# A hybrid transformer block: turned tiles in groups of four, a longer lead in the expert stage, and gathers issued singly

## The reference, cut to what matters

```python
x = x + attn_a(ln(x))   # rope attention, 16 heads of 8
x = x + ffn(ln(x))
x = x + attn_b(ln(x))   # covariance attention, 16 heads of 8
x = x + ffn(ln(x))
# ffn: h = x + attention(layer_norm(x)); h + moe_ff(layer_norm(h))
def moe_ff(x, w_gate, w1, b1, w2, b2):
    t = x.reshape(B * T, D)                          # 2048 rows of 128
    tw, ti = lax.top_k(softmax(t @ w_gate), 2)       # of 8 experts
    tw = tw / jnp.sum(tw, axis=-1, keepdims=True)
    for e in range(8):
        we = jnp.sum(jnp.where(ti == e, tw, 0.0), axis=-1)
        h = gelu(t @ w1[e] + b1[e]) @ w2[e] + b2[e]  # 128 -> 512 -> 128
        out = out + we[:, None] * h
```

## Time and profile before

| | |
|---|---|
| median of 3 runs | 967.03 us (964.18 to 973.73) |
| profiled execution | 970.91 us |
| its span | 969.1 us |
| PE busy | 803.9 us (83%) |
| ACT, DVE, POOL busy | 576.6, 545.4, 481.1 us |
| PE's mean granted clock | 0.871 |
| mixture of phase 1 | 328.6 to 482.4 us |
| mixture of phase 2 | 798.5 to 941.4 us |

### The profile page before, as it was taken

How to read it: one execution, slowest core, us unless ns; L and a number is a source line. 1 busy time by engine, 2 the same in 40 slices (tenths; PEclk the granted TensorE clock), 3 DMA queues, 4 the chain that set the end, 5 groups by cost and what they waited for, 6 DMA issues and landing times.

```text
span 969.1 us, 21562 instructions
## 1 busy us (share of the span) xinstructions
PE 803.9 (83%) x7166; PEld 574.7 (59%) x7166; DVE 545.4 (56%) x1370; ACT 576.6 (60%) x1336; POOL 481.1 (50%) x906
## 2 busy tenths in 40 slices
PE   2999999999985983879878989999998599666780
PEld 2755556666652783878745556666665258566680
DVE  4799988788872230023656768788887322210122
ACT  1377767878752681555555556787876248444460
POOL 6667777577635215045444456366763621412305
PEclk9999989999965896889978889999998558878895
DMA  9200000000001452555200000000000124435552
GB/s 288 68 3 2 3 2 3 3 3 3 3 13 34 121 155 84 134 147 147 59 13 13 14 13 2 3 2 3 3 3 5 42 75 126 132 101 154 145 135 65
DMA packets 58746, 56.31 MB, mean 58 GB/s; under 512 B 7944, under 2 KB 43536, under 8 KB 58640
## 3 DMA queue, kind: packets, MB, share of 16 engines
q1 hardware_dynamic: 40288, 39.13, 15.0%
q0 software_dynamic: 4096, 8.40, 3.0%
q10 hardware_dynamic: 14256, 7.41, 2.6%
HBM read 40.10 MB, written 14.29 MB: 56 GB/s over the span
## 4 chain that ended last, share of the span: by engine, by line
PE 56%; DVE 17%; POOL 8%; issue 7%; another core or an unknown queue 7%; ACT 4%; DMA 1%; ACTq 1%; POOLq 0%; DVEq 0%; SPq 0%
PE bankO L456 11%; DVE M L1112 9%; PE bankE L697 8%; PE bankR L710 8%; PE bankE L475 7%; PE bankE L429 6%; PE bankR L442 3%; POOL Yg L1610 3%; DVE QKV L1074 2%; PE bankE L466 2%; ACT G L951 2%; PE bankR L526 2%; PE bankR L544 2%; PE bankR L496 1%
## 5 line engine op out<-in xcount | busy, mean ns | idle before, releaser
L1112 DVE TENSOR_REDUCE M<-bankR 128x2 f32<-128x512 f32 x512 | 326.5, 684 | 113.1 <-PE bankR L442 76.9
L838 ACT ACTIVATE Pr<-bankE 128x512 f32<-128x512 f32 x512 | 276.9, 595 | 128.2 <-PE bankE L429 119.8
L442 PE MATMUL bankR<-KQ 32*128 32x256 f32 x1024 | 181.6, 349 | 17.5 <-DVE M L1112 13.7
L456 PE MATMUL bankO<-Pr,Vx 128*32 128x256 f32 x2048 | 179.7, 427 | 5.9 <-ACT OT L832 5.9
L429 PEld LDWEIGHTS bankE<-KQ 32*128 32x128 f32 x1024 | 85.3, 199 | 108.7 <-issue 72.4
L1327 DVE COPY Yb<-bankR 128x128 f32<-128x128 f32 x92 | 26.6, 290 | 208.7 <-PE bankR L710 137.5
L429 PE MATMUL bankE<-KQ 32*128 32x256 f32 x1024 | 141.6, 350 | 1.7 <-issue 0.6
L951 ACT ACTIVATE G<-bankE,W 128x128 f32<-128x128 f32 x368 | 105.0, 371 | 56.7 <-PE bankE L697 35.6
L442 PEld LDWEIGHTS bankR<-KQ 32*128 32x128 f32 x1024 | 117.2, 198 | 32.2 <-DVE M L1112 27.3
L710 PE MATMUL bankR<-w,G 128*128 x736 | 107.9, 294 | 27.0 <-ACT G L951 23.7
L1610 POOL DMA_INDIRECT Yg<-sorted_y,SLOT x64 | 61.8, 966 | 126.6 <-DMA sorted_y<-Yb 97.3
(11 more groups left out here) (169 smaller groups left out, 1169.4 us busy)
## 6 DMA issues: line engine op xcount, KB each, us to landing
W<-in_w1b SPq DMA_DIRECT2D x92, 258.0 KB
XT<-sorted_u SPq DMA_DIRECT2D x92, 64.0 KB
sorted_y<-Yb ACTq DMA_DIRECT2D x92, 64.0 KB
sorted_u<-Yg SPq DMA_DIRECT2D x2, 1472.0 KB, 9.6
KQ<-MT SPq DMA_DIRECT2D x128, 4.0 KB
X<-in_x SPq DMA_DIRECT2D x8, 128.0 KB, 6.5
sorted_u<-U,SLOT POOLq DMA_INDIRECT x64
Yg<-sorted_y,SLOT POOLq DMA_INDIRECT x64
```

Of the source, the lines that this page charges most:

```text
L442: k = mm(dve_bank("raw", layer, b, h)[:, z * T:z * T + T], QT[rows, kb, g, z * P:z * P + P], KT[rows, kb, g, :], start=True, stop=True)
L456: k = mm(bankO[SL * j:SL * j + SL, cols], Vx[:, b % VB, kc, HG * g + j, :], Pr[:, g % 2, j, kc, :], start=(g % 2 == 0 and kc == 0), stop=( ...
L838: nc.scalar.activation(Pr[:, (h // HG) % 2, h % HG], act_bank("S", layer, b, h).rearrange("p (k q) -> p k q", k=TT), ACT.Exp, scale=EXP_SC ...
L1112: v.tensor_reduce(M[:, b % 2, :, h], dve_bank("raw", layer, b, h).rearrange("p (t k) -> p t k", t=TT), AX.X, ALU.max, negate=True).then_in ...
```

## The change

- The tiles are turned in groups of XG = 4 (the last group of a half has 3), 6 groups to a half. SP loads a group with one DMA, PE turns its tiles into one bank of bankE, ACT copies the bank at once. XT and XTT hold two groups.
- PE's `hidden` runs LEAD = 3 tiles ahead of `outputs`, ACT's gelu two ahead; G holds 5 tiles, W 7, Yb 6. ACT stores tile `at - 4`. Each half begins anew with two turned groups and three `hidden`.
- SP asks for W 7 tiles ahead across the border of the halves, and for the second half's first groups at tile 18.
- `timely` goes: block 5 has its gate in step 18, blocks 6 and 7 in `drain`. `first_rows` and `name_tiles` are one with `sort_rows`. For half 0, `do_rank` part 0 stands at the end of step 17 and part 1 with the sort in step 18; the scatter of half 0 follows step 18. For half 1 all stand one tile later.
- In the steps, `do_uT`, `do_gate`, `choose` and `weigh` stand somewhat later on every engine. In `fill`, seven pairs of raw scores and maxima stand at tiles 16 to 22 of the second half, combines of blocks 2 and 3 at 17 and 20.
- The four gathers of a covariance step are issued one by one: before `stack_k`, after it, after `stack_v` and after `norm`.

```diff
@@ -40,7 +40,13 @@
 GROUPS = HB * TT * 2
 NTL = (GROUPS * P + E * (P - 1)) // P
 NAT = 2 * NTL
-NX, NW, NY, NYG = 6, 5, 3, 8
+LEAD = 3
+LAG = 4
+NXG, NW, NGB, NY, NYG = 2, 7, 5, 6, 8
+XG = 4
+GROUP = [(half * NTL + i, min(XG, NTL - i)) for half in range(2) for i in range(0, NTL, XG)]
+NGRP = len(GROUP)
+GROUP_OF = {first: q for q, (first, _) in enumerate(GROUP)}
 
 
...
 
-        def timely(u):
-
-            return None if u and LAYERS[u[0]] == "ffn" and u[1] >= NB - 3 else u
+        def group_at(at):
+
+            return GROUP_OF.get(at + XG + 2) if at % NTL + XG + 2 < NTL else None
+
+        def group_of(at):
+
+            q = max(q for q, (first, _) in enumerate(GROUP) if first <= at)
+            return q, at - GROUP[q][0]
...
 
-            def load_x(ph, at):
-
-                half, i = divmod(at, NTL)
-                k = (ph * NAT + at) % NX
+            def load_x(ph, q):
+
+                half, i = divmod(GROUP[q][0], NTL)
+                n, k = GROUP[q][1], (ph * NGRP + q) % NXG
                 if i == 0:
                     sp.wait_ge(scattered[half], 16 * GROUPS * (ph + 1))
-                need(sp, x_turned, ph, at - NX)
-                sp.dma_start(XT[:, k], sorted_u[half][i * P:i * P + P, :]).then_inc(x_in[k], 16)
+                need(sp, x_turned, ph, q - NXG)
+                sp.dma_start(XT[:, k, 0:n, :],
+                             sorted_u[half][i * P:(i + n) * P, :].rearrange("(j p) d -> p j d", p=P)).then_inc(x_in[k], 16)
 
             def load_w(ph, at):
...
                         set_shift(*m, 0)
-                def begin(half):
-                    for i in range(NW - 1):
-                        load_w(ph, half * NTL + i)
-                    for i in range(NX - 1):
-                        load_x(ph, half * NTL + i)
-
-                for half in range(2):
-                    begin(half)
-                    for i in range(NTL):
-                        at = half * NTL + i
-                        if i + NX - 1 < NTL:
-                            load_x(ph, at + NX - 1)
-                        if i + NW - 1 < NTL:
-                            load_w(ph, at + NW - 1)
+                for at in range(NW):
+                    load_w(ph, at)
+                for q in range(2 * NXG):
+                    load_x(ph, q)
+                for at in range(NAT):
+                    if at + NW < NAT:
+                        load_w(ph, at + NW)
+                    if group_at(at - 1) is not None and group_at(at - 1) % (NGRP // 2) < NGRP // 2 - NXG:
+                        load_x(ph, group_at(at - 1) + NXG)
+                    if at == NTL - XG - 1:
+                        for q in range(NGRP // 2, NGRP // 2 + 2 * NXG):
+                            load_x(ph, q)
 
             dst = out.rearrange("b (t p) d -> p b t d", p=P)
             for b in range(NB):
...
                     do_mT(*a, 1)
-                if ranks:
-                    do_rank(m[0] // 2, 0, 0)
+                if a and LAYERS[a[0]] == "ffn" and a[1] == NB - 1:
+                    do_rank(a[0] // 2, 0, 1)
                 if t:
...
 
-            def turn_x(ph, at):
-                n = ph * NAT + at
-                pe.wait_ge(x_in[n % NX], 16 * (n // NX + 1))
-                ring_e.take(pe, ("x", ph, at))
-                turn(act_bank("x", ph, at)[:, 0:P], XT[:, n % NX, :], ident[:]).then_inc(x_turned.sem, 1)
-                ring_e.give(("x", ph, at), x_copied, ph, at)
+            def turn_x(ph, q):
+                x = ph * NGRP + q
+                pe.wait_ge(x_in[x % NXG], 16 * (x // NXG + 1))
+                ring_e.take(pe, ("x", ph, q))
+                for j in range(GROUP[q][1]):
+                    k = turn(act_bank("x", ph, q)[:, j * P:j * P + P], XT[:, x % NXG, j, :], ident[:])
+                k.then_inc(x_turned.sem, 1)
+                ring_e.give(("x", ph, q), x_copied, ph, q)
 
             def hidden(ph, at):
                 n = ph * NAT + at
-                need(pe, x_copied, ph, at)
+                q, j = group_of(at)
+                if j == 0:
+                    need(pe, x_copied, ph, q)
                 pe.wait_ge(w1_in[n % NW], 16 * (n // NW + 1))
                 ring_e.take(pe, ("hid", ph, at))
                 for c in range(FC):
                     k = mm(act_bank("hid", ph, at)[:, c * P:c * P + P], W1[:, n % NW, c * P:c * P + P],
-                           XTT[:, n % 2, :], start=True, stop=True)
+                           XTT[:, (ph * NGRP + q) % 2, j, :], start=True, stop=True)
                 k.then_inc(hid.sem, 1)
...
-                turn_x(ph, 0)
-                turn_x(ph, 1)
-                hidden(ph, 0)
-                for at in range(NAT):
-                    if at + 2 < NAT:
-                        turn_x(ph, at + 2)
-                    if at + 1 < NAT:
-                        hidden(ph, at + 1)
-                    outputs(ph, at)
-                    drain(ph, at)
-                    if ph == 0:
-                        fill(layer + 1, at - NTL)
+                for half in range(2):
+                    turn_x(ph, half * NGRP // 2)
+                    turn_x(ph, half * NGRP // 2 + 1)
+                    for at in range(half * NTL, half * NTL + LEAD):
+                        hidden(ph, at)
+                    for at in range(half * NTL, half * NTL + NTL):
+                        if at % NTL + LEAD < NTL:
+                            hidden(ph, at + LEAD)
+                        outputs(ph, at)
+                        if group_at(at) is not None:
+                            turn_x(ph, group_at(at))
+                        drain(ph, at)
+                        if ph == 0:
+                            fill(layer + 1, at - NTL)
...
+                    if s == STEPS - DRAIN - 2:
+                        do_rank(ph, 0, 0)
                 mixture(ph)
 
...
-
-                need(act, x_turned, ph, at)
-                need(act, hid, ph, at - 2)
-                nc.scalar.activation(XTT[:, (ph * NAT + at) % 2, :], act_bank("x", ph, at)[:, 0:P], ACT.Identity,
-                                     bias=lncols[:, 3:4], scale=lncols[:, 2:3]).then_inc(x_copied.sem, 1)
+            def copy_x(ph, q):
+
+                n = GROUP[q][1]
+                need(act, x_turned, ph, q)
...
             def mixture(ph):
                 layer = 2 * ph + 1
+                do_weT(ph, 0)
                 do_pv(layer, NB - 1, 1)
-                do_weT(ph, 0)
                 do_weT(ph, 1)
                 do_onT(layer, NB - 1)
-                copy_x(ph, 0)
-                copy_x(ph, 1)
-                hidden(ph, 0)
-                for at in range(NAT):
-                    if at + 2 < NAT:
-                        copy_x(ph, at + 2)
-                    if at + 1 < NAT:
-                        hidden(ph, at + 1)
-                    if at:
-                        store(ph, at - 1)
-                    drain(ph, at)
-                    if ph == 0:
-                        fill(layer + 1, at - NTL)
-                store(ph, NAT - 1)
+                for half in range(2):
+                    for x in range(2):
+                        copy_x(ph, half * NGRP // 2 + x)
+                        hidden(ph, half * NTL + x)
+                    for at in range(half * NTL, half * NTL + NTL):
+                        if at % NTL + 2 < NTL:
+                            hidden(ph, at + 2)
+                        if group_at(at) is not None:
+                            copy_x(ph, group_at(at))
+                        if at >= LAG:
+                            store(ph, at - LAG)
+                        drain(ph, at)
+                        if ph == 0:
+                            fill(layer + 1, at - NTL)
+                for at in range(NAT - LAG, NAT):
...
                     turn(*n, 1)
-                if ranks:
-                    sort_rows(m[0] // 2, 0)
                 if t:
                     divide(*t)
                 if m == (0, 0):
@@ -1197,12 +1185,6 @@
                     do_max(*m, 4)
                 if rope:
                     rotate(*n, 0, 1)
-                if ranks:
-                    name_tiles(m[0] // 2, 0)
-                if u:
-                    do_gate(*u)
-                if block_of(u) is not None:
-                    choose(*block_of(u))
                 if late(p):
                     combine(0, p[1])
                     norm_in(*p)
@@ -1213,12 +1195,14 @@
                 if rope:
                     rotate(*n, 2, 0)
                     rotate(*n, 2, 1)
-                if block_of(gone) == (0, 0) or block_of(gone) == (1, 0):
+                if u:
+                    do_gate(*u)
+                if block_of(gone) is not None:
                     weigh(*block_of(gone))
+                if block_of(u) is not None:
+                    choose(*block_of(u))
                 if m:
                     do_max(*m, 6)
-                if block_of(u) == (0, 1) or block_of(u) == (1, 1):
```

(14 more changed lines are left out.)

## The result

The changed kernel takes 913.43 us (median of 4 runs, 910.85 to 914.91), the kernel before 966.04 beside it (964.18 to 973.73): a ratio of 0.9438, 95% interval 0.9382 to 0.9494. The forecast was 918, range 898 to 955.

The account below looks back on a forecast made before the run. PE's late signals in runs of indirect DMAs and the chain through GpSimd to the norm were taken to cost the time. Terms -20 - 19 - 14 + 4 = -49 us from 970.9 gave 922, less 3.9 for the median: 918, range 898 to 955.

Parts of the forecast that it names:

- Covariance steps: Four covariance steps: single gathers, at least two of four, leave the way to the norm; -14 us, ends 0 and -16.7.
- Mixture phase 2: Phase 2's mixture stage: less PE idle time in pauses and less half clock, -20 us in all.
- Phase 1: Phase 1's mixture stage: the same pauses, -20, and +1 for block 3's fourth gather behind a norm; -19 us.
- Scatter of half 1: In the mixture: of 13.9 us of PE pauses the lead, spent once, saves two tiles' time; -4 us, bounds 0 and -8.
- Rival (a): Runs of indirect DMAs: PE's late signals are the bound and the lead hides nothing; 941 us, chance 0.22.
- Gathers in a row: Eight gathers in the mixture: PE pauses of 4.2 and 2.4 us fall under the lead's cover; -4.5 us, bounds 0 and -6.5.
- Table loads, small pauses: In the mixture: two 1.3 us pauses behind ACT's table loads vanish, -2.7; 6.7 us of small pauses shrink, -3.
- Border: Between the mixture's halves: XT asked for early, but refill and W of tile 26 cost 2.8 us; -1, bounds -3 and +4.
- Late scatter: Half 0's scatter after step 18, starting near 304: the stall moves unshrunk, x just in time; +2 us per phase, +4.
- Rival (d): Ahead of the mixtures: half 0's late scatter is exposed, up to +12 us per phase; 938 us, chance 0.06.
- Rival (c): Covariance steps: every indirect DMA by itself holds PE's signals for 2.6 us; slower by 24, 991 us, chance 0.08.
- (e): Single gathers: GpSimd's descriptor writing waits beside DVE, 0.27 us per gather; 922 us, chance 0.04.

Follow-up runs that it names:

- e1: The kernel before, with only the covariance steps' four gathers issued singly between GpSimd's other work: 946.35 us, ratio 0.9746 to the kernel before.
- e3: The changed kernel with the four gathers of a covariance step in a row ahead of the norm again: 932.18 us, ratio 0.9593 to the kernel before.
- e4: The changed kernel with PE's lead of `hidden` back at one tile instead of three: 915.6 us, ratio 0.9432 to the kernel before.
- e9: The changed kernel with both halves' scatters in fours and two memsets (1.6 us of GpSimd) between them: 892.52 us, ratio 0.9235 to the kernel before.
- e2: The kernel before, with only the scatter of half 0 issued after step 18 instead of step 17: 964.63 us, ratio 0.9959 to the kernel before.
- e6: The changed kernel with one memset ahead of each of the 16 gathers of blocks 0 to 3 in phase 2: 913.47 us, ratio 0.9473.
- e10: The changed kernel with both halves' scatters in fours and one memset (0.8 us) between them: 909.81 us, ratio 0.9423 to the kernel before.
- e5: The changed kernel with half 1's scatter in fours and four memsets (3.15 us) between them: 909.85 us, ratio 0.9443 to the kernel before.
- e12: e11 with the mixtures' gathers in fours too, by the norm in phase 1 and two memsets in phase 2: 878.2 us, ratio 1.0077 in its own series.
- e11: e9 with the mixture's drain work up to half 1's sort two tiles earlier: 881.36 us, ratio 0.9117 to the kernel before.

## Why the prediction was right, and which steps failed

The total was off by 5 us; a look at the steps is less kind.

- **Covariance steps**, -14: measured -15.5, and e1 and e3 give 14.0 and 14.7 alone. The norm 10.6 us after QKV, as foreseen. What was missed: the same edit gains 4.9 us in the fill of phase 1, which I had put at nothing behind the mixture.
- **Mixture phase 2**, -20: measured -16.9 from tile 0 on. **Phase 1**, -19: -13.2, of which 4.9 are the gathers of the fill, so 8.3 by the named terms. By the prediction's own marks, from the first L697/L707 to the last output, it is -15.7 and -12.0: 127.1 and 141.0 us, where it had said about 123 and 135. Both were missed, by 4 and 6 us. The terms inside were wrong:
  - *Scatter of half 1, -4, "the lead is spent once and saves two tiles' time"*: this step failed. The six tiles gave 3.0 and 2.4 us, and e4 shows 0.7 and 0.4 of them for the lead. PE's idle time in it did fall to 10.1 us, the "near 10" of the prediction, from 15.0; but it is now spread between held starts, at a granted clock of 0.71, and against the 13.8 us of e9 at 1.00 the stretch still loses 16 us. Rival (a) had the mechanism nearly right: what PE does ahead helps little, since PE's own starts are held.
  - *Gathers in a row, -4.5*: failed too. Tiles 26 to 34 take 0.4 us more in phase 2 and 3.6 more in phase 1, there with the store's lag of four tiles and the wait of 9.52 us for the norm, a cost of the change that the prediction had at nothing.
  - *Table loads, small pauses*, -2.7 and -3: tiles 0 to 12 gave 4.8 and 6.5 us, the largest gain beside the fill. There the matmuls fell (243 to 224 in phase 1), PE's busy time with them by 2.8 us, and idle from 2.9 to 0.9 us. Six of those matmuls are block 5's gate, gone from the stage; twelve (a turned WE and a b2) only stand later, in tiles 18 to 26. No pause stands before L720 behind a table load, as foreseen, and e4 shows that this is the lead's doing. But the moved side work, which the prediction had at 0, is the larger part of what this stretch shows.
  - *Last tiles of phase 2* (34 to 45), with no term of their own: -5.6. PE's idle time fell from 2.8 to 0.1 us, a wait of 2.27 for the copied XTT above all; of the rest 1.8 is the `hidden` of two tiles that the lead moved ahead of tile 34.
  - *Border*, -1: tiles 18 to 26 gave 2.5 and 2.8, inside the bounds. A W load of 4.65 us stands in the chain there, but PE waits for it only 0.9 us; the sign of 4 us didn't come.
  - *Clock*, -5: granted 0.90 and 0.87 for 0.87 and 0.84. Its price wasn't measured apart; e9 has the scatter's stretch at 1.00.
- **Late scatter**, +4: measured -2.6 and -6.7 ahead of the mixtures, and e2 gives -3 for the move alone, little more than two traces differ by. The failed step was the start "near 304": rank and sort were ready at 291, so x was never late; the first turn came 12 us after the scatter's end, not within 4. Rival (d) falls.
- **Rival (c)**, single DMAs hold PE, falls by e1, and by e6 where they stand 1.9 us apart. **(e)**: the gathers take 940 to 1098 ns, median 950, where the earlier trace rows had 940 to 1210, median 944. The Trainium skill's port lock (SBUF — State Buffer, "SBUF: two separate sides") shows no price in these durations. The Trainium skill says there that a DVE operation with two SBUF inputs takes this lock only against GpSimd work that reads SBUF, which the prediction left out. The prediction's 16 x 2.5 us was also the example's difference, not its factor.
- The tail and the ffn steps: 0 and -1.2, as foreseen.

That the total came out is in good part luck: a term that the prediction had put at nothing (the fill), one with the wrong sign (the stretch ahead of the mixtures) and side work gone from the first tiles made up for what the lead did not do. Of the large terms only the covariance steps came out for the reason given.

## What to carry to other kernels

When an engine's signals are late under a run of indirect DMAs, look whether a lead lets it work or only shows it held in another way: cut both traces at equal work and compare the stretch, not the pauses. Here a run broken every four DMAs by 1.7 us of other GpSimd work gave PE 16 us back per scatter; if the order allows, put such DMAs singly between other work, and start them early, for their end comes later. Then look who waits for that end: in e6 PE was free of the DMAs and lost the same time to a DVE that waited for their data. A lag added to stores delays whoever waits for the last of them, and that wait can be on the engine that the lag was to free.

## What the runs showed of the hardware

- PE under a run of GpSimd's indirect DMAs 1.27 us apart: free for about 6 us (five DMAs), then one to three matmuls per 1.4 us until some 3 us after the run's end. The same 117 matmuls take 29.7 us in the changed kernel, 13.9 with 3.3 us free after each four DMAs, 13.8 with 1.7, 27.3 with 0.9. Gathers 1.88 us apart, 0.9 of it free, leave PE its nine matmuls per us.
- ACT's last wait for a signal of PE ends 22.9 us after the start of 16 DMAs in the kernel before (360.20 to 383.08), 22.8 in the changed one (356.25 to 379.01), and 17.0 after the start of 12 gathers (842.9 to 859.93 in phase 2): 1.42 or 1.43 us per DMA each time. As an estimate from these, something works off one DMA per 1.42 us and PE waits for it to catch up: it can't in a run (1.27), barely or not in e10 (1.40), and can in e9 (1.55), e5 and e6 (1.88). The numbers fit; no run was made to test it. What it is that is held, whether the taking of the trace has a part in it, and whether an idle GpSimd would do as well as memsets, wasn't tried.
- It isn't always there, it seems: in one series of five the kernel before took 874 us in place of 966, with a granted clock of 0.90 to 0.94 for 0.86 to 0.89. No trace of it was taken, so where those 92 us went stays open. e12, which has all edits of the changed kernel and the pauses, took 878 beside it: in that case all of them together gained nothing. Neither the changed kernel nor e11 was run then, so how much of the 5.6% is left is open too.
